# TensorE takes a step's logits ahead of its shared parts, and one part behind the ranks; four groups' statistics move behind group 1's routing

## The chip, the cores and the metric

One NeuronCore of a Trainium2 chip runs the whole program in one launch. The metric is the device time of an execution in microseconds (us); all times below are us unless marked otherwise. The engines are PE (TensorE, matmuls; PEld is its weight load), DVE (VectorE), ACT (ScalarE), POOL (GpSimd) and SP (SyncE, here a DMA queue). Each takes its own instructions in the order of the program and waits on semaphores for the others.

## The reference

x is 4096 tokens of 128 values (16 x 256 x 128). Three sublayers follow each other: a mixture of experts at half weight, a decaying scan between two circular convolutions, and the same mixture of experts again, with the same weights.

```python
def ffn(x_):                                   # x_ is 4096 x 128
    logits = x_ @ router.T                     # 8 experts
    onehot = one_hot(argmax(logits))           # one expert for each token
    y  = sum over e of onehot[:, e] * ((silu(x_ @ gate[e].T) * (x_ @ up[e].T)) @ down[e].T)
    ys = (silu(x_ @ w_gate_s.T) * (x_ @ w_up_s.T)) @ w_down_s.T      # shared expert, every token
    return y + ys
x = x + 0.5 * ffn(layernorm(x))
x = x + attn(layernorm(x))    # x + gate * circ_corr(scan(circ_conv(x, bind)), unbind)
x = x + 0.5 * ffn(layernorm(x))
```

All data are float32. A hidden width is 256, so the gate and up projections of one expert are two halves of 128 each.

## The kernel before

The 4096 tokens are 32 tiles of 128, held as 8 groups of 4 tiles (512 tokens); a group g has its columns in every buffer. Each of the two mixtures (f = 0 and f = 1) has a routing stage, which walks over the groups in steps k = 0 to 7, and an expert stage over blocks of 128 tokens sorted by expert.

A step k of the routing stage does the following for group k. PE multiplies the turned rows by the router (`logits`, L899). DVE finds the best expert (`choose`, L648 to L654; `chosen` is the one-hot choice). PE counts with small matmuls which place each token has among those of its expert (`ranks`, L918 to L926). DVE makes row numbers from them (`place_rows`, L663 and L667, tile `slot`). POOL then sends the four tiles with four indirect DMAs, the scatters (L349), to the buffer `dispatched`. In the same step ACT normalizes the next group (`norm`, L430), PE turns it (`turn`, L860, into one PSUM bank), and ACT copies the turned bank out (`evac_rows`, L445, tile `xnT`), which the next step's logits read.

The shared expert fills the gaps. For each group it has three parts: (g, 0) and (g, 1) are the two halves of gate and up (PE L874, then `silu` on ACT L454, then a product on DVE L623), and (g, DOWN) is the down projection (PE L882, then an addition on DVE L591). The list SHARED_PARTS sets their order, two to a step. I call the first part of a step A and the second B:

| step k | 1 | 2 | 3 | 4 | 5 | 6 | 7 |
|---|---|---|---|---|---|---|---|
| A | (0,0) | (1,0) | (1,1) | (1,DOWN) | (3,0) | (3,1) | (3,DOWN) |
| B | (0,1) | (0,DOWN) | (2,0) | (2,1) | (2,DOWN) | (4,0) | (4,1) |

The order within a step is written out by hand for each engine, in a function `front(f, k)` of its own. On PE it was: A, logits, B, turn of group k+1, ranks. On ACT, which the change leaves alone, it is: `evac_rows` of group k, `norm` of group k+1, silu of A, silu of B. The silu of a step's B is thus ahead of the copy that the next step's logits wait for.

In the second mixture (f = 1) the step also carries the scan. On PE, behind the logits, stands the product of the scanned rows with `mix` (L905, waits for DVE's scan L603), and at the end of the step the turn of group k+3 for the scan. On DVE the step is: scan of group k+2, the addition of returned expert rows (L591), `choose`, A's product, the addition of the retrieved rows (`add_retrieved`, L610), the statistics of that group (L550 to L561), `place_rows`, B's product. POOL has two reciprocal square roots (L338) ahead of a step's four scatters.

Behind step 7 DVE makes the tables of the expert blocks (`pads_behind` L736, then from `n_up` L749 to `tab_row` L777); five more shared parts stand ahead of the first expert matmul on PE (L951).

In the first mixture the mean and variance of groups 4 to 7 (`stats_of`) were taken on DVE in step 0 and step 1, because their load of x (`x_in[3]`) lands late. Newton steps in step 2 then make their reciprocal square roots.

Of the kernel before, what the change touches and what calls it, by code (L numbers as in the profile page):

```python
# [22 lines left out]
G = NT // TPG  # L23
# [29 lines left out]
LATE_ROWS = 4  # L53
# [7 lines left out]
def build(nc, x_in, gu_in, dn_in, router_in, bind_in, unbind_in, gate_in, decay_in, out):  # L61
# [6 lines left out]
    with ExitStack() as ctx:  # L68
# [152 lines left out]
        def valid(k):  # L221
            return 0 <= k < G
# [317 lines left out]
        def _(dve):  # L540
# [128 lines left out]
            def front(f, k):  # L669
                n, q = f * G + k, k % 2  # L670

                kind, later = ("f", G - 1 if k == 1 else G) if f == 0 else ("a", k + 4)
                if f == 0 and k == -AHEAD:
                    dve.wait_ge(x_in[0], 16)
                    stats_of("f", 0, 0)
                if f == 0 and k == 1 - AHEAD:
                    dve.wait_ge(x_in[1], 16)
                    stats_of("f", 1, 1)
                if f == 0 and k == 2 - AHEAD:
                    dve.wait_ge(x_in[2], 16)  # L680
                    stats_of("f", 2, 2)
                    stats_of("f", 3, 3)
                if valid(k):
                    root = f == 0 and k == 2
                    choose(n, q, kind, later, later, root)
                    if root:
                        for i in range(ROUTE_STEPS - 2, NEWTON_STEPS):
                            newton_step(i)
                for g, part in parts_at(k, 0):
                    shared(f, g, part)  # L690
                if f == 1 and valid(k + 2):
                    add_retrieved(k + 2)
                    stats_of("f", n + 2, k + 2)
                if valid(k):
                    place_rows(n, k, q)
                if f == 0 and k == 0:
                    dve.wait_ge(x_in[3], 16)
                    for late in range(G - LATE_ROWS, G - 1):
                        stats_of("f", late, late)
                if k == G - 1:  # L700
                    pads_behind(f)
                for g, part in parts_at(k, 1):
                    shared(f, g, part)
# [150 lines left out]
        def _(pe):  # L854
# [31 lines left out]
            def front(f, k):  # L886
                n, q = f * G + k, k % 2
                if n == 1:
                    pe.wait_ge(shared_in, 16 * 2)
                for g, part in parts_at(k, 0):  # L890
                    shared(f, g, part)
                if valid(k):
                    if n == 0:
                        pe.wait_ge(router_ready, 16)
                        pe.wait_ge(const_made, N_CONST)
                    pe.wait_ge(xnT_ready, n + 1)
                    wait_pos(pe, route, n * ROUTE_STEPS)
                    for t in range(TPG):
                        last = nc.tensor.matmul(rt[:, t * E:(t + 1) * E], xnT[:, k, t * P:(t + 1) * P], routerT[:],  # L899
                                                start=True, stop=True)  # L900
                    last.then_inc(logits, 1)
                if f == 1 and valid(k + 2):
                    pe.wait_ge(scan_done, k + 3)
                    for t in range(TPG):
                        last = nc.tensor.matmul(tp["a"][:, t * C:(t + 1) * C], scanned[:, q, t * P:(t + 1) * P],  # L905
                                                mix[:], start=True, stop=True)
                    last.then_inc(mixed, 1)
                for g, part in parts_at(k, 1):
                    shared(f, g, part)
                if valid(k + 1):  # L910
                    turn("f", n + 1, xn, k + 1, xnT_ready)
                if valid(k):

                    pe.wait_ge(route, n * ROUTE_STEPS + ROUTE_STEPS - 1)
                    if k == G - 1:
                        count_all()
                    ranks = by_tile(rt[:, RANK])
                    nc.tensor.matmul(ranks, before[:], chosen[:, q, 0:TPG, :], start=True, stop=False)  # L918
                    for t in range(TPG - 1):
                        nc.tensor.matmul(ranks[:, t + 1:TPG, :], ones[:],  # L920
                                         chosen[:, q, t:t + 1, :].to_broadcast([P, TPG - 1 - t, E]),
                                         start=False, stop=False)
                    nc.tensor.matmul(ranks, ones[:], chosen[:, q, TPG:TPG + 1, :].to_broadcast([P, TPG, E]),
                                     start=False, stop=False)

                    nc.tensor.matmul(ranks, ones[:], region[:].unsqueeze(1).to_broadcast([P, TPG, E]),  # L926
                                     start=False, stop=True).then_inc(ranked, 1)
                if f == 1 and valid(k + 3):
                    turn("a", k + 3, xa, 1 - q, x2_done)

# [110 lines left out]
```

## Time and profile before

| what | value |
|---|---|
| median of 3 runs | 297.3 (297.2 to 298.74) |
| the profiled execution | 297.33 |
| its span, first to last instruction | 295.6 |
| busy: PE, DVE, ACT, POOL | 254.9, 189.0, 160.5, 178.7 |
| mean granted clock of PE | 0.961 |

The profiled execution has 1.7 outside its span and stands at the median of the runs. The busy times are sums over stages with different limits; which engine ends last has to be read from each stage. The stages lie in the span about as follows: routing of the first mixture to 60, its experts from 66 to 127, the scan and the routing of the second mixture to 210, its experts from 216.

### The profile page before, as it was taken

Reading aid. Unit: us, or ns where it says so; the run is one execution under the profiler, and the core shown is the slowest. Engines: PE = TensorE matmul, PEld = TensorE weight load, DVE = VectorE, ACT = ScalarE, POOL = GpSimd, SP = SyncE. Lnnn points to the kernel's source line nnn. Section 1 sums busy time; section 2 is a strip of 40 time slices with the busy share of each in tenths; the row PEclk is TensorE's granted clock in tenths of the full one; section 3 lists DMA queues with packets and bytes.
Section 4 is the critical chain, followed back from the end, with each engine's and each line's share of the span. In section 5 each row is a group of like instructions: output and inputs, shape, how many; then the busy total and the mean of one; then the engine's idle time right before and its main releaser. Section 6 shows DMA issues by size and latency. Waiting matters only on the chain.

```text
span 295.6 us, 6436 instructions
## 1 busy us (share of the span) xinstructions
PE 254.9 (86%) x1788; PEld 211.0 (71%) x1788; DVE 189.0 (64%) x734; ACT 160.5 (54%) x374; POOL 178.7 (60%) x260
## 2 busy tenths in 40 slices
PE   0799999969999999985589988999779999999940
PEld 0557777648999999845466767766369999999520
DVE  4695665864555555448996999867625566565362
ACT  2705545145767767326497877750447767775100
POOL 6555677722777777723457788877307758887400
PEclk9999999999999999997676999999999999999995
DMA  6970111323344321147000001112323434311297
GB/s 187 332 300 27 48 55 59 95 79 74 102 111 107 105 81 47 45 130 185 0 1 27 29 28 38 49 45 83 96 64 104 107 94 111 90 54 48 65 303 237
DMA packets 34996, 28.42 MB, mean 96 GB/s; under 512 B 4784, under 2 KB 31792, under 8 KB 34704
## 3 DMA queue, kind: packets, MB, share of 16 engines
q1 hardware_dynamic: 25328, 16.06, 19.7%
q0 software_dynamic: 4544, 9.45, 9.7%
q10 hardware_dynamic: 5088, 2.50, 2.9%
q8 instruction: 14, 0.23, 0.4%
q14 instruction: 22, 0.18, 0.2%
HBM read 15.37 MB, written 12.62 MB: 95 GB/s over the span
## 4 chain that ended last, share of the span: by engine, by line
POOL 33%; PE 22%; issue 19%; DMA 10%; DVE 9%; ACT 2%; SPq 2%; POOLq 0%; DVEq 0%; ACTq 0%
POOL dispatched L349 15%; POOL returned L378 12%; PE bank L951 10%; PE bank L959 4%; PE bank L874 4%; DMA ey<-returned 4%; POOL scale_f L338 2%; DMA xres<-in_x 2%; POOL token L372 2%; DMA dispatched<-xn,slot 2%; DMA returned<-ey,token 2%; DVE st_f L550 1%; DMA xs<-dispatched 1%; SPq L308 1%; PE bank L899 1%
## 5 line engine op out<-in xcount | busy, mean ns | idle before, releaser
L378 POOL DMA_INDIRECT returned<-ey,token x78 | 76.8, 985 | 32.8 <-issue 17.8
L951 PE MATMUL bank<-xsT,wgu 128*128 128x128 f32 x624 | 83.0, 276 | 2.4 <-ACT xsT L497 2.4
L349 POOL DMA_INDIRECT dispatched<-xn,slot x64 | 63.5, 992 | 24.6 <-issue 17.7
L951 PEld LDWEIGHTS bank<-xsT,wgu 128*128 128x128 f32 x624 | 75.7, 192 | 3.4 <-ACT xsT L497 1.7
L874 PE MATMUL bank<-xnT,gu 128*128 128x512 f32 x128 | 66.7, 649 | 3.6 <-DVE hs L623 2.8
L805 DVE COPY ey<-bank 128x128 f32<-128x128 f32 x78 | 22.7, 292 | 45.6 <-PE bank L959 45.6
L481 ACT ACTIVATE wgu<-gu 128x512 f32 x78 | 48.3, 623 | 4.1 <-issue 3.9
L454 ACT ACTIVATE sg<-bank 128x512 f32<-128x512 f32 x32 | 18.9, 592 | 54.7 <-PE bank L874 47.3
L959 PE MATMUL bank<-wdn,eh 128*128 128x128 f32 x312 | 47.5, 276 | 0.5 <-DVE eh L800 0.5
L503 ACT ACTIVATE eg<-bank 128x256 f32<-128x256 f32 x78 | 29.8, 383 | 32.6 <-PE bank L951 32.4
L959 PEld LDWEIGHTS bank<-wdn,eh 128*128 128x128 f32 x312 | 40.9, 192 | 0.9 <-DVE eh L800 0.9
L874 PEld LDWEIGHTS bank<-xnT,gu 128*128 128x128 f32 x128 | 23.5, 203 | 23.5 <-issue 22.3
L882 PEld LDWEIGHTS bank<-dn,hs 128*128 128x128 f32 x256 | 31.0, 196 | 9.5 <-DVE hs L623 8.1
L882 PE MATMUL bank<-dn,hs 128*128 128x128 f32 x256 | 32.8, 282 | 4.7 <-DVE hs L623 4.7
L800 DVE TENSOR_TENSOR eh<-eg,bank 128x256 f32<-128x256 f32 x78 | 32.1, 411 | 5.9 <-ACT eg L503 5.9
L430 ACT ACTIVATE xn<-xres,shift_f,scale_f 128x128 f32<-128x128 f32 x64 | 26.3, 483 | 15.7 <-POOL shift_f L342 15.7
L623 DVE TENSOR_TENSOR hs<-sg,bank 128x512 f32<-128x512 f32 x32 | 21.8, 682 | 13.0 <-ACT sg L454 12.8
L786 DVE COPY wdn<-dn 128x256 f32 x78 | 23.6, 303 | 3.0 <-issue 3.0
L899 PEld LDWEIGHTS bank<-routerT,xnT 128*128 128x128 f32 x128 | 18.6, 215 | 7.3 <-issue 6.9
L860 PE MATMUL bank<-ident,xn 128*128 128x128 f32 x64 | 12.7, 319 | 7.7 <-POOL before L405 7.5
L860 PEld LDWEIGHTS bank<-ident,xn 128*128 128x128 f32 x64 | 9.4, 163 | 13.8 <-POOL before L405 7.5
L899 PE MATMUL bank<-routerT,xnT 128*128 128x8 f32 x128 | 17.5, 263 | 0.9 <-ACT xnT L445 0.8
(102 smaller groups left out, 282.7 us busy)
## 6 DMA issues: line engine op xcount, KB each, us to landing
xs<-dispatched SPq DMA_DIRECT2D x80, 66.0 KB, 1.9
ey<-returned SPq DMA_DIRECT2D x16, 256.0 KB, 5.7
gu<-in_gu SPq DMA_DIRECT2D x1, 2048.0 KB, 11.3
out<-xres ACTq DMA_DIRECT2D x8, 256.0 KB, 4.2
returned<-ey,token POOLq DMA_INDIRECT x78
dn<-in_dn SPq DMA_DIRECT2D x1, 1024.0 KB, 11.7
dispatched<-xn,slot POOLq DMA_INDIRECT x64, 2.3
dispatched<-pads SPq DMA_DIRECT2D x10, 66.0 KB
```

The lines of the kernel that those rows point to most:

```text
L349: nc.gpsimd.indirect_dma_start(dispatched[:, :], bass.IndirectOffsetOnAxis(slot[:, i:i + 1], 0), xn[:, i, :], None, bounds_check=last_row) ...
L378: nc.gpsimd.indirect_dma_start(returned[:, :], bass.IndirectOffsetOnAxis(token[:, b:b + 1], 0), ey[:, b, :], None, bounds_check=last_back) ...
L430: nc.scalar.activation(dst[:, at * TPG + t, 0:C], xres[:, i, :], ACT.Identity, bias=shift[kind][:, i:i + 1], scale=scale[kind][:, i:i + 1] ...
L481: nc.scalar.activation(wgu[:, b % WR, :], tile(gu, expert_of(digits[0], b)), ACT.Copy).then_inc(blk_wgu, 1)
L503: nc.scalar.activation(eg[:, b % WR, :], bank[4 + b % WR][:, 0:H], ACT.Silu).then_inc(blk_silu, 1)
L786: nc.vector.tensor_copy(wdn[:, b % WR, :], tile(dn[:].rearrange("p e h c -> p e (h c)"), expert_of(digits[0], b)))
L800: nc.vector.tensor_tensor(eh[:, b % WR, :], eg[:, b % WR, :], bank[4 + b % WR][:, H:2 * H], ALU.mult).then_inc(blk_mul, 1)
L874: last = nc.tensor.matmul(ps[:], gu[:, SHARED, at:at + P], xnT[:, g, :], start=True, stop=True)
L882: last = nc.tensor.matmul(o_ps[:, t * C:(t + 1) * C], hs[:, n % 2, h, t * P:(t + 1) * P], dn[:, SHARED, h, :], start=(h == 0), stop=(h == ...
L899: last = nc.tensor.matmul(rt[:, t * E:(t + 1) * E], xnT[:, k, t * P:(t + 1) * P], routerT[:], start=True, stop=True)
L951: last = nc.tensor.matmul(bank[4 + b % WR][:, i * P:(i + 1) * P], wgu[:, b % WR, i * P:(i + 1) * P], xsT[:, b // 2 % 2, b % 2, :], start=T ...
L959: last = nc.tensor.matmul(y_of(b), eh[:, b % WR, h * P:(h + 1) * P], wdn[:, b % WR, h * C:(h + 1) * C], start=(h == 0), stop=(h == HH - 1))
```

## The change

On PE, the logits of a step now come first (with the product by `mix`, where there is one); then A, then the turn and the ranks, and B behind the ranks. In step 1 of the first mixture both parts stand behind the ranks. On DVE, only step 1 of the first mixture changes, and step 0's three sets of statistics move: group 4's are taken between the instructions of step 1's `choose`, groups 5 and 6's behind its `place_rows`, then A's product, then group 7's. ACT, POOL and SP have the same instructions in the same order.

```diff
 # DVE
-                kind, later = ("f", G - 1 if k == 1 else G) if f == 0 else ("a", k + 4)
+                kind, later = ("f", G - LATE_ROWS if k == 1 else G) if f == 0 else ("a", k + 4)
...
                 if valid(k):
+                    if n == 1:
+                        dve.wait_ge(x_in[3], 16)
                     root = f == 0 and k == 2
                     choose(n, q, kind, later, later, root)
...
-                for g, part in parts_at(k, 0):
-                    shared(f, g, part)
+                if n != 1:
+                    for g, part in parts_at(k, 0):
+                        shared(f, g, part)
...
-                if f == 0 and k == 0:
-                    dve.wait_ge(x_in[3], 16)
-                    for late in range(G - LATE_ROWS, G - 1):
+                if n == 1:
+                    for late in range(G - LATE_ROWS + 1, G - 1):
                         stats_of("f", late, late)
+                    for g, part in parts_at(k, 0):
+                        shared(f, g, part)
+                    stats_of("f", G - 1, G - 1)
 # PE
-                for g, part in parts_at(k, 0):
-                    shared(f, g, part)
                 if valid(k):
...
-                for g, part in parts_at(k, 1):
-                    shared(f, g, part)
+                if n != 1:
+                    for g, part in parts_at(k, 0):
+                        shared(f, g, part)
                 if valid(k + 1):
                     turn("f", n + 1, xn, k + 1, xnT_ready)
...
+                if n == 1:
+                    for g, part in parts_at(k, 0):
+                        shared(f, g, part)
+                for g, part in parts_at(k, 1):
+                    shared(f, g, part)
                 if f == 1 and valid(k + 3):
                     turn("a", k + 3, xa, 1 - q, x2_done)
```

PE before, step 3 of the first mixture and the head of step 4 (`xnT,gu` is a gate part, `dn,hs` a DOWN part, `routerT,xnT` the logits, `ident,xn` the turn, `chosen,before` the first of the ranks):

```order
L874 MATMUL bank<-xnT,gu 128x512 x2
L899 MATMUL bank<-routerT,xnT 128x8 x4
L874 MATMUL bank<-xnT,gu 128x512 x2
L860 MATMUL bank<-ident,xn 128x128 x4
L918 MATMUL bank<-chosen,before 128x32
L920 MATMUL bank<-chosen,ones 128x24
L920 MATMUL bank<-chosen,ones 128x16
L920 MATMUL bank<-chosen,ones 128x8
L923 MATMUL bank<-chosen,ones 128x32
L926 MATMUL bank<-region,ones 128x32
L882 MATMUL bank<-dn,hs 128x128 x8
L899 MATMUL bank<-routerT,xnT 128x8 x4
```

The same stretch of PE now:

```order
L902 MATMUL bank<-routerT,xnT 128x8 x4
L879 MATMUL bank<-xnT,gu 128x512 x2
L865 MATMUL bank<-ident,xn 128x128 x4
L922 MATMUL bank<-chosen,before 128x32
L924 MATMUL bank<-chosen,ones 128x24
L924 MATMUL bank<-chosen,ones 128x16
L924 MATMUL bank<-chosen,ones 128x8
L927 MATMUL bank<-chosen,ones 128x32
L930 MATMUL bank<-region,ones 128x32
L879 MATMUL bank<-xnT,gu 128x512 x2
L902 MATMUL bank<-routerT,xnT 128x8 x4
L887 MATMUL bank<-dn,hs 128x128 x8
```

Between B's last matmul and the logits of step 4, where step 4's A stood, nothing stands any more.

ACT in the same stretch, the same before and now: the copy of group 3's turned rows (`xnT`), the norm of group 4, step 3's two silus (`sg`, the second is B's), the copy of group 4's turned rows:

```order
L445 ACTIVATE xnT<-bank 128x512 [waits turned_f]
L430 ACTIVATE xn<-xres,shift_f,scale_f 128x128 [waits late_rstd]
L430 ACTIVATE xn<-xres,shift_f,scale_f 128x128 x3
L454 ACTIVATE sg<-bank 128x512 [waits mult_done,gu_done] x2
L445 ACTIVATE xnT<-bank 128x512 [waits turned_f]
```

The copy that the logits wait for stood and stands behind B's silu; only what PE has to do meanwhile has moved.

PE in the second mixture, step 2 before (`mix,scanned` is the product that waits for the scan):

```order
L874 MATMUL bank<-xnT,gu 128x512 [waits mult_done,xnT_ready]
L874 MATMUL bank<-xnT,gu 128x512
L899 MATMUL bank<-routerT,xnT 128x8 [waits route,xnT_ready]
L899 MATMUL bank<-routerT,xnT 128x8 x3
L905 MATMUL bank<-mix,scanned 128x128 [waits scan_done]
```

and now:

```order
L902 MATMUL bank<-routerT,xnT 128x8 [waits route,xnT_ready]
L902 MATMUL bank<-routerT,xnT 128x8 x3
L908 MATMUL bank<-mix,scanned 128x128 [waits scan_done]
L908 MATMUL bank<-mix,scanned 128x128 x3
L879 MATMUL bank<-xnT,gu 128x512 [waits mult_done,xnT_ready]
```

A gate part that stood ahead of the wait for the scan stands behind it.

## Rows read from the trace of the kernel before

**Rows 1.** The page, chain of work that ended last, shares of the span by line.
```profile
POOL dispatched L349 15%; POOL returned L378 12%; PE bank L951 10%; PE bank L959 4%; PE bank L874 4%; DMA ey<-returned 4%; POOL scale_f L338 2%; DMA xres<-in_x 2%; POOL token L372 2%; DMA dispatched<-xn,slot 2%; DMA returned<-ey,token 2%; DVE st_f L550 1%; DMA xs<-dispatched 1%; SPq L308 1%; PE bank L899 1%
```

**Rows 2.** Timeline, POOL's scatters: start, duration, engine, line; idle before, and its releaser.
```profile
24.27 0.97 POOL L349 DMA_INDIRECT dispatched<-xn,slot  x1 [4.54 <-DVE slot L667]
...
30.32 0.97 POOL L349 DMA_INDIRECT dispatched<-xn,slot  x1 [1.27 <-DVE slot L667]
...
59.88 0.97 POOL L349 DMA_INDIRECT dispatched<-xn,slot  x1 [0.30 <-issue]
```

**Rows 3.** Timeline, PE and DVE in steps 0 to 2 of the first mixture.
```profile
13.78 3.76 PE L874 MATMUL bank<-xnT,gu 128*128 128x512 f32 x4
13.97 0.19 DVE L663 TENSOR_TENSOR place<-bank,chosen 128x32 f32<-128x32 f32 x1 [0.44 <-PE bank L926]
...
15.91 0.87 DVE L550 BATCH_NORM_STATS2 st_f<-xres 128x6 f32<-128x128 f32 x4
...
17.33 1.72 PE L899 MATMUL bank<-routerT,xnT 128*128 128x8 f32 x8
...
20.58 0.22 DVE L654 TENSOR_REDUCE chosen<-chosen 128x8 bf16<-128x40 bf16 x1
...
23.69 1.88 PE L874 MATMUL bank<-xnT,gu 128*128 128x512 f32 x4
...
25.41 0.95 PE L899 MATMUL bank<-routerT,xnT 128*128 128x8 f32 x8
```

**Rows 4.** Timeline, PE and ACT in step 6 of the first mixture.
```profile
46.17 0.95 PE L899 MATMUL bank<-routerT,xnT 128*128 128x8 f32 x8
...
46.98 1.96 PE L874 MATMUL bank<-xnT,gu 128*128 128x512 f32 x4
...
48.78 0.60 PE L860 MATMUL bank<-ident,xn 128*128 128x128 f32 x4
...
48.98 0.60 ACT L454 ACTIVATE sg<-bank 128x512 f32<-128x512 f32 x1 [1.96 <-PE bank L874]
...
49.37 2.03 PE L882 MATMUL bank<-dn,hs 128*128 128x128 f32 x16
...
49.47 0.59 ACT L445 ACTIVATE xnT<-bank 128x512 f32<-128x512 f32 x1
...
51.24 0.96 PE L899 MATMUL bank<-routerT,xnT 128*128 128x8 f32 x8
```

**Rows 5.** The page, costliest groups: DVE's product of a gate part (busy, mean ns).
```profile
L623 DVE TENSOR_TENSOR hs<-sg,bank 128x512 f32<-128x512 f32 x32 | 21.8, 682 | 13.0 <-ACT sg L454 12.8
```

**Rows 6.** Timeline, first mixture's tables and the shared part behind them.
```profile
55.28 0.16 DVE L749 TENSOR_SCALAR n_up<-bank 128x8 int32<-128x8 f32 x1
...
60.92 1.95 PE L874 MATMUL bank<-xnT,gu 128*128 128x512 f32 x4 [1.43 <-DVE hs L623]
```

**Rows 7.** Timeline, DVE and PE in steps 1, 2 and 5 of the second mixture.
```profile
160.26 0.19 DVE L648 TENSOR_REDUCE top<-bank 128x4 f32<-128x32 f32 x1 [2.24 <-issue]
...
162.95 0.68 DVE L610 TENSOR_TENSOR xres<-bank,xres 128x512 f32<-128x512 f32 x1
...
167.32 1.16 PE L905 MATMUL bank<-mix,scanned 128*128 128x128 f32 x8 [0.47 <-DVE scanned L603]
...
168.31 1.95 PE L882 MATMUL bank<-dn,hs 128*128 128x128 f32 x16
...
170.56 0.68 DVE L610 TENSOR_TENSOR xres<-bank,xres 128x512 f32<-128x512 f32 x1
...
191.34 0.68 DVE L610 TENSOR_TENSOR xres<-bank,xres 128x512 f32<-128x512 f32 x1
```

**Rows 8.** Timeline, second mixture, PE: turn of the second tile for the experts.
```profile
214.96 0.33 PE L940 MATMUL bank<-ident,xs 128*128 128x128 f32 x1 [0.92 <-DMA xs<-dispatched]
```

**Rows 9.** Windows: length; busy PE, PEld, DVE, ACT, POOL; PEclk (granted clock), DMA, GB/s.
```profile
151.00:152.00 1.00, 0.93 (x8) 0.93 (x8) 0.97 (x5) 0.64 (x2) 0.60 (x1) 1.00 0.00 0
...
153.00:154.00 1.00, 0.99 (x8) 0.65 (x8) 0.94 (x8) 1.00 (x3) 0.11 (x1) 0.50 0.00 0
```

## The prediction

> **What bounds the kernel now.** I read the chain of work that ended last first: POOL's scatters hold 15% of the span [rows 1], and all of them lie in the two routing stages, so these stages are where the change has to be weighed. Next I read POOL in the timeline [rows 2]. In the first mixture it stands idle twice, 4.54 us before group 1's first scatter and 1.27 before group 2's, each time for DVE's row numbers. From 30.32 on it never waits: the 24 scatters of groups 2 to 7 start at 30.32 to 59.88, 29.56 / 23 = 1.285 each, or 5.14 for a group. So the most that can be won there is the two waits less the 0.30 that POOL needs between scatters anyway: 4.24 + 0.97 = 5.2.
>
> Then I read the timeline of PE over one step [rows 4]. From the logits of step 6 to those of step 7 it is 51.24 - 46.17 = 5.07: logits 0.81, A (a gate part) 1.80, turn and ranks 0.59, B (a DOWN part) 1.87. PE has no gap in it. The reader should see that PE's 5.07 is nearly POOL's 5.14. A step that grows by more than a few tenths makes POOL wait again, and what is lost in several steps adds up.
>
> **First mixture, the gain at the start.** Before, group 1's logits stood behind (0, 0), a part of 17.33 - 13.78 = 3.55 us [rows 3]. That part took twice what a gate part takes later (1.80), so PE ran there at the lower of its two clock levels. Now the logits follow group 0's ranks. They must wait until DVE has read these (13.97 + 0.19), so they start at about 14.3. From logits to the end of `choose` took 20.80 - 17.33 = 3.47, with the same interleaved statistics and the same clock, so group 1's choice is there at 17.8 and its row numbers about 1 us later, before POOL is through with group 0's scatters at 24.27 - 4.54 = 19.73. The 4.54 wait goes.
>
> **First mixture, group 2.** Behind the ranks, from about 18.0, PE does (0, 0) and (0, 1). At the lower clock both end at 18.0 + 7.1 = 25.1. Before, PE was slow in (0, 1) and fast in the part at 23.69; if the clock returns at the same time, near 23.2, they end at about 24.1; if it returns as early as the start of (0, 1), at 23.35. Now the new wait comes in. Group 2's logits read the copy that ACT makes of the turned rows, and on ACT that copy stands behind the silu of (0, 1). From the rows of step 6 [rows 4]: the silu starts 2.00 after a gate part's start (48.98 - 46.98), the copy 0.49 after the silu (49.47), and it ends 0.59 later, 3.08 after the part's start. PE is through with the part after 1.80. So whenever B is a gate part, PE stands idle for 3.08 - 1.80 = 1.3 us. Before, A of the next step filled this time. Group 2's logits then come at 24.1 + 1.3 = 25.4, against 25.41 [rows 3]: no change, bounds 24.65 and 26.4 from the two ends above. What is behind the logits (choice, Newton steps, row numbers) is as before, so POOL's second wait remains, and the time won on group 1 is waited away there: gain 0, bounds -0.8 and +1.0.
>
> The moved statistics I cost at nothing. Groups 5 and 6 run on DVE while PE does (0, 0), group 7 while it does (0, 1); DVE then waits for group 2's logits in any case. The wait for the late load of x stands later than before, where the late groups' statistics ran at 15.91 already. If that cover went, group 2 would be late by what is left of one set, whose four statistics take 0.87 and their aggregation about as much.
>
> **First mixture, steps 3 to 7.** B is a gate part in steps 3, 4 and 6, so the logits of steps 4, 5 and 7 each come 1.3 later: 3.9 by step 7. PE's other work per step is the same. POOL, with its 5.14 against PE's 5.07, can't make it up. DVE is not late on its own: it gets the choice done under A.
>
> **First mixture, the end.** Before, step 7's B, (4, 1), ran between its logits and its ranks; now it runs behind the last ranks, and DVE still makes its product ahead of the tables. Before, tables came 55.28 - 51.24 = 4.04 after the logits of step 7 [rows 6, 4]. Now it is logits 0.81, (3, DOWN) 1.87, ranks 0.15, then 2.00 to the silu, 0.60 for it, 0.68 for the product [rows 5]: 6.1. That adds 2.1. Behind the tables PE waits for DVE (1.43 at 60.92), so the shared parts there and the first expert matmul behind them move along [rows 6]. Sum of the first mixture: 0 + 3.9 + 2.1 = +6.0.
>
> **Second mixture.** DVE's step goes by `add_retrieved`: 162.95, 170.56, ..., 191.34 for steps 1 to 5, 28.4 for four steps [rows 7]. Now A stands on PE behind the product with `mix`, which waits for DVE's scan, and DVE needs A's result ahead of `add_retrieved`. The loop closes: from `add_retrieved` over the scan to the `mix` product 167.32 - 162.95 = 4.37, product 168.31 - 167.32 = 0.99, gate part to silu 2.00, silu 0.60, product 0.68 [rows 4, 5]: 8.6 for steps 2, 3 and 5. Step 4 has a DOWN part, 1.87 and 0.2 to its end in place of part and silu: 8.1. Four steps are 33.9, 5.5 more than before. Step 1 starts it: DVE can take its choice up to 2.24 earlier (its wait before 160.26), but its next product now needs (0, 0), which PE does last instead of first. I take 0, bounds -2.2 and +1.75 (a gate part at the lower clock less one at the higher). The end costs 2.1 as above, less the 0.92 for which PE waited there for data anyway [rows 8]: +1.2. Sum of the second mixture: +6.7.
>
> **The clock.** At 151 to 152 PE did only logits and `mix` products, 0.93 busy, at full granted clock; at 153 to 154 the granted clock was 0.50 [rows 9]. Now every step from 2 to 5 has such a stretch of some 4 us between B and A: turn, copy, logits, the wait for the scan, product. I take one of the five A parts of steps 1 to 5 at half clock: +1.75; none is the lower bound, all five the upper. The page "TensorE: Matmul & The Clock Gate" of the Trainium skill, section "Why this matters for your kernels", says that gaps between bursts of matmuls in mid-kernel throw PE back to its slow clock, which speaks against this change; by it all five parts would be slow, and that is the second rival below. These rows show one such fall; none shows it for gaps of this very mix.
>
> **The sum**, against the profiled execution's 297.33, which is the median: 297.33 + 6.0 + 6.7 + 1.75 = 311.8. Expert stages and the final stores have the same instructions and no new wait: 0.
>
> **Rivals.**
> 1. Only the first mixture loses. In the second, POOL has a step of its own (four scatters and two square roots); if DVE's product comes before it needs it, because the choice runs 2 us earlier, the loop doesn't close. 297.33 + 6.0 = 303.3. Against it: 8.6 is made of durations that follow each other on different engines, and the step of before, 7.6, had PE and DVE nearly full.
> 2. PE's clock falls in every step. All five A parts at 1.75 more: 297.33 + 6.0 + 6.7 + 8.75 = 318.8. For it, rows 9; against it, PE still has two heavy parts in each step.
> 3. The change gains: the copy comes in time, and PE's step stays within POOL's 5.14, so that POOL's two waits are won for good: 297.33 - 5.2 = 292.1. It decides where the copy ends before PE has finished B. That needs it ahead of B's silu on ACT, and the program has it behind.
> 4. The gain at the start and the new waits cancel in the first mixture, and the second is bound by POOL as before: 297.
>
> **How the numbers follow.** Forecast 311.8, chance 0.56, its own range 307 to 316 (step 1's and group 2's bounds). Rival 1: 0.14. Rival 2: 0.20. Rival 3: 0.06. Rival 4: 0.04. The range 303 to 319 leaves out rivals 3 and 4 and the far side of rival 2, about 2 in 10. About 0.5%, 1.5 us, is what a measurement of this kernel can tell from no change. Faster 0.06, same 0.04, slower 0.90.
>
> **What would show it.** In the trace of after: group 1's scatters directly behind group 0's, and a wait of some 5 us ahead of group 2's; PE waiting about 1.3 for ACT's copy ahead of the logits of groups 2, 4, 5 and 7 in the first mixture and POOL waiting in steps 4 to 7; the tables' first instruction near 61; in the second mixture `add_retrieved` every 8.6 with DVE waiting for ACT's silu ahead of A's product. The prediction is wrong if PE's logits don't wait for the copy, or if DVE's wait for A's product is absent, or if PE's granted clock falls much oftener than once.

## The result, and the profile after

| | before | after |
|---|---|---|
| median of the runs made side by side | 297.41 | 319.31 |
| ratio, 95% interval | | 1.0763 [1.0701, 1.0825] |
| the profiled execution, its span | 297.33, 295.6 | 319.95, 318.2 |
| mean granted clock of PE | 0.961 | 0.924 |
| first expert matmul of the first and of the second mixture | 66.27, 215.96 | 74.59, 238.48 |

One execution of the changed kernel took 660.69, twice the others (318.48 to 319.95); the median of 319.31 counts it, the ratio does not. The change made the kernel 7.6% slower by the ratio. The median is 7.5 above the forecast of 311.8 and 0.3 above the upper end of the range; the three others lie on both sides of that end.

The first expert matmuls, two of the kernel before and two of the changed one, in the timeline of PE:

```profile
66.27 2.02 PE L951 MATMUL bank<-xsT,wgu 128*128 128x128 f32 x16 [0.68 <-ACT xsT L497]
215.96 2.02 PE L951 MATMUL bank<-xsT,wgu 128*128 128x128 f32 x16 [0.68 <-ACT xsT L497]
...
74.59 2.05 PE L960 MATMUL bank<-xsT,wgu 128*128 128x128 f32 x16 [1.09 <-DVE xres L591]
238.48 1.72 PE L960 MATMUL bank<-xsT,wgu 128*128 128x128 f32 x13 [1.14 <-DVE xres L591]
```

By these, the first mixture lost 74.59 - 66.27 = 8.3, and from there to the same point in the second it took 163.9 where it took 149.7, so 14.2 were lost there. What follows costs 0.1 more. The first expert stage is as long as before (58.2 against 58.3). Thus the two routing stages hold the whole loss.

The page of the changed kernel, the chain that ended last by engine and by line, against [rows 1]:

```profile
PE 40%; DVE 16%; issue 15%; POOL 14%; DMA 6%; ACT 4%; SPq 2%; DVEq 1%; POOLq 0%; ACTq 0%
PE bank L879 13%; POOL returned L378 11%; PE bank L960 9%; PE bank L887 6%; PE bank L902 4%; PE bank L968 4%; DMA ey<-returned 3%; DVE st_f L550 3%; PE bank L908 2%; POOL token L372 2%; DMA xres<-in_x 2%; ACT sg L454 2%; DVE xres L610 2%; D
```

The scatters (L349), 15% of the chain before, have no entry in the line; in their place stand PE's gate and DOWN parts (L879, L887) and the engines that hand results to each other. So POOL no longer sets the end of the routing stages. POOL's timeline in the first mixture, the scatters that waited for DVE's row numbers, against [rows 2]:

```profile
28.93 0.97 POOL L349 DMA_INDIRECT dispatched<-xn,slot  x1 [4.67 <-DVE slot L667]
...
42.19 0.97 POOL L349 DMA_INDIRECT dispatched<-xn,slot  x1 [3.26 <-DVE slot L667]
49.28 0.97 POOL L349 DMA_INDIRECT dispatched<-xn,slot  x1 [2.29 <-DVE slot L667]
...
60.73 0.97 POOL L349 DMA_INDIRECT dispatched<-xn,slot  x1 [1.56 <-DVE slot L667]
```

Group 1's wait of 4.54 is gone. A wait of 4.67 stands ahead of group 2, and POOL then waits 3.26, 2.29 and 1.56 ahead of groups 4, 5 and 7, where before it never did; groups 3 and 6, with 0.39 and 0.31, are hardly over the 0.30 that lies between scatters anyway. The reason is in the timeline of PE and ACT at the end of step 3 and in step 4, against [rows 4]:

```profile
33.16 1.96 PE L879 MATMUL bank<-xnT,gu 128*128 128x512 f32 x4
35.16 0.60 ACT L454 ACTIVATE sg<-bank 128x512 f32<-128x512 f32 x1 [2.62 <-PE bank L879]
35.65 0.59 ACT L445 ACTIVATE xnT<-bank 128x512 f32<-128x512 f32 x1
...
36.30 1.06 PE L902 MATMUL bank<-routerT,xnT 128*128 128x8 f32 x8 [1.18 <-ACT xnT L445]
37.21 3.27 PE L887 MATMUL bank<-dn,hs 128*128 128x128 f32 x16
40.27 1.05 PE L865 MATMUL bank<-ident,xn 128*128 128x128 f32 x4
```

Read it downwards: B ends, ACT takes its silu, only then the copy, and PE stands still for 1.18 until the copy is there. The same 1.18 stands ahead of the logits at 44.45 and 55.96, and 0.96 ahead of those at 23.95. What the prediction did not have is the next row: the DOWN part behind the wait took 3.27, where one takes 1.95 to 2.03. The windows of these microseconds (columns as in [rows 9]) show the granted clock:

```profile
32.00:33.00 1.00, 0.34 (x5) 0.11 (x2) 0.86 (x6) 0.54 (x1) 0.69 (x2) 1.00 0.00 0
...
35.00:36.00 1.00, 0.12 (x1) 0.00 (x0) 0.21 (x1) 0.84 (x2) 0.69 (x2) 1.00 0.23 72
36.00:37.00 1.00, 0.70 (x7) 0.70 (x7) 0.47 (x1) 1.00 (x4) 0.69 (x2) 1.00 0.08 30
37.00:38.00 1.00, 1.00 (x10) 1.00 (x10) 0.54 (x3) 0.77 (x3) 0.69 (x2) 0.88 0.12 38
38.00:39.00 1.00, 1.00 (x7) 1.00 (x7) 0.64 (x4) 0.00 (x0) 0.93 (x1) 0.50 0.20 68
...
40.00:41.00 1.00, 1.00 (x7) 1.00 (x6) 0.48 (x1) 0.00 (x0) 0.00 (x0) 0.50 0.00 0
```

PE was busy for 0.34 of the microsecond from 32 (its ranks waited 0.66 for DVE's choice), fully from 33 to 35, for 0.12 and 0.70 of the next two, and then its granted clock fell from 1.00 to 0.50, its lower level of 1.2 GHz, and stayed there through the DOWN part.

In the second mixture the timeline shows one whole turn of the loop that the prediction describes, against [rows 7]:

```profile
172.75 0.68 DVE L610 TENSOR_TENSOR xres<-bank,xres 128x512 f32<-128x512 f32 x1
...
175.27 1.03 PE L902 MATMUL bank<-routerT,xnT 128*128 128x8 f32 x8 [0.96 <-DVE place L663]
175.86 1.21 DVE L603 TENSOR_TENSOR_SCAN scanned<-keep,bank 128x512 f32<-128x512 f32 x1
...
177.13 1.57 PE L908 MATMUL bank<-mix,scanned 128*128 128x128 f32 x8 [0.82 <-DVE scanned L603]
...
178.49 3.20 PE L879 MATMUL bank<-xnT,gu 128*128 128x512 f32 x4
...
181.72 0.60 ACT L454 ACTIVATE sg<-bank 128x512 f32<-128x512 f32 x1 [3.64 <-PE bank L879]
...
182.35 0.69 DVE L623 TENSOR_TENSOR hs<-sg,bank 128x512 f32<-128x512 f32 x1 [2.49 <-ACT sg L454]
...
182.95 0.68 DVE L610 TENSOR_TENSOR xres<-bank,xres 128x512 f32<-128x512 f32 x1
```

From `add_retrieved` to the next is 10.20: 4.38 to the product with `mix`, 1.36 to A, 3.23 to its silu, 0.63 to DVE's product, 0.60 to `add_retrieved`. DVE waits 2.49 for the silu. The forecast for the same links was 4.37, 0.99, 2.00, 0.60 and 0.68, in all 8.64. So the loop is the one described, and what is too long in it is what PE does. Windows:

```profile
174.00:175.00 1.00, 0.31 (x3) 0.07 (x1) 0.93 (x9) 1.00 (x3) 0.00 (x0) 1.00 0.00 0
...
176.00:177.00 1.00, 0.30 (x3) 0.21 (x2) 1.00 (x2) 1.00 (x4) 0.76 (x3) 1.00 0.00 0
177.00:178.00 1.00, 0.87 (x6) 0.88 (x7) 0.97 (x5) 1.00 (x3) 0.70 (x2) 0.85 0.00 0
178.00:179.00 1.00, 1.00 (x5) 0.82 (x4) 1.00 (x8) 0.08 (x1) 0.89 (x1) 0.50 0.21 68
```

The granted clock falls at the product with `mix`, reads 0.50 in the microsecond in which A begins, and is back at 1.00 when B runs. A is slow in all of steps 1 to 5: the gate parts at 168.33, 178.49, 188.66 and 208.11 took 3.16 to 3.30, and the DOWN part at 198.83 took 3.28. But step 1's A was slow in the kernel before, too:

```profile
155.37 3.62 PE L874 MATMUL bank<-xnT,gu 128*128 128x512 f32 x4
```

There the granted clock was 0.50 from 153 to 159. So four slow parts are new, those of steps 2 to 5.

### The profile page after: what moved, and what is told of

Same layout as the page of the kernel before. It is cut to its first block, busy times and chain, and to the rows that moved or that the text cites. A ratio compares the mean times of both kernels' runs of the same rounds, so it can differ in the third digit from the quotient of the medians.

```text
span 318.2 us, 6435 instructions
## 1 busy us (share of the span) xinstructions
PE 266.0 (84%) x1788; PEld 217.9 (68%) x1788; DVE 189.8 (60%) x734; ACT 160.5 (50%) x374; POOL 178.8 (56%) x260
## 4 chain that ended last, share of the span: by engine, by line
PE 40%; DVE 16%; issue 15%; POOL 14%; DMA 6%; ACT 4%; SPq 2%; DVEq 1%; POOLq 0%; ACTq 0%
PE bank L879 13%; POOL returned L378 11%; PE bank L960 9%; PE bank L887 6%; PE bank L902 4%; PE bank L968 4%; DMA ey<-returned 3%; DVE st_f L550 3%; PE bank L908 2%; POOL token L372 2%; DMA xres<-in_x 2%; ACT sg L454 2%; DVE xres L610 2%; DVE xres L591 1%; DMA returned<-ey,token 1%
## 5 line engine op out<-in xcount | busy, mean ns | idle before, releaser
L349 POOL DMA_INDIRECT dispatched<-xn,slot x64 | 63.3, 989 | 30.1 <-issue 16.5
L879 PE MATMUL bank<-xnT,gu 128*128 128x512 f32 x128 | 69.0, 673 | 4.2 <-DVE hs L623 3.4
L623 DVE TENSOR_TENSOR hs<-sg,bank 128x512 f32<-128x512 f32 x32 | 21.9, 684 | 38.9 <-ACT sg L454 38.9
L879 PEld LDWEIGHTS bank<-xnT,gu 128*128 128x128 f32 x128 | 25.2, 215 | 27.4 <-issue 26.3
L887 PEld LDWEIGHTS bank<-dn,hs 128*128 128x128 f32 x256 | 34.3, 214 | 8.8 <-DVE hs L623 7.9
L887 PE MATMUL bank<-dn,hs 128*128 128x128 f32 x256 | 36.4, 302 | 4.1 <-DVE hs L623 4.1
L902 PEld LDWEIGHTS bank<-routerT,xnT 128*128 128x128 f32 x128 | 17.9, 217 | 17.7 <-ACT xnT L445 13.9
L902 PE MATMUL bank<-routerT,xnT 128*128 128x8 f32 x128 | 19.0, 275 | 12.2 <-ACT xnT L445 7.3
L338 POOL TENSOR_TENSOR scale_f<-var_f,minus_half 128x4 f32<-128x4 f32 x12 | 12.2, 1015 | 19.2 <-DVE minus_mean_f L561 19.2
L865 PEld LDWEIGHTS bank<-ident,xn 128*128 128x128 f32 x64 | 10.5, 180 | 15.0 <-POOL before L405 7.4
```

The lines of the kernel that those rows point to most:

```text
L349: nc.gpsimd.indirect_dma_start(dispatched[:, :], bass.IndirectOffsetOnAxis(slot[:, i:i + 1], 0), xn[:, i, :], None, bounds_check=last_row) ...
L879: last = nc.tensor.matmul(ps[:], gu[:, SHARED, at:at + P], xnT[:, g, :], start=True, stop=True)
L887: last = nc.tensor.matmul(o_ps[:, t * C:(t + 1) * C], hs[:, n % 2, h, t * P:(t + 1) * P], dn[:, SHARED, h, :], start=(h == 0), stop=(h == ...
```

## The experiments

Each kernel is compared with the kernel before on the same chip (medians 296.55 to 296.77 there). A profile shows a single execution; where that one is far from its kernel's median, the text says so.

**1. The copy taken earlier.** ACT copies the next group's turned rows ahead of B's silu, in both mixtures; everything else as in the changed kernel.

```diff
 # ACT, front(f, k)
-                if valid(k):
+                if valid(k) and k < 2:
                     evac_rows(n)
...
+                if 1 <= k < G - 1:
+                    evac_rows(n + 1)
                 for g, part in parts_at(k, 1):
                     shared(f, g, part)
```

> ACT copies the next group's turned rows ahead of the silu of the step's B, in both mixtures; nothing else differs from the changed kernel. Theory (in the first mixture PE waits for that copy, 1.2 us at each of groups 4, 5 and 7, and the lower clock in two DOWN parts follows from these waits): the first mixture's steps go back to 5.07, its first expert matmul from 74.6 to about 68.5, the second mixture stays within 1 us, whole time about 313. Rival A (the logits are late for something else, such as DVE's row numbers): no change, 319. Rival B (the copy also sets the second mixture's loop): about 306.

Measured: 309.18 (308.65 to 310.4), ratio 1.0415 [1.0348, 1.0483]. The first expert matmul came at 66.07, so all of the first mixture's 8.3 was back, more than the 6 expected. The timeline of PE and ACT in steps 3 and 4:

```profile
31.30 0.59 ACT L445 ACTIVATE xnT<-bank 128x512 f32<-128x512 f32 x1
...
31.98 1.96 PE L881 MATMUL bank<-xnT,gu 128*128 128x512 f32 x4
33.78 0.95 PE L904 MATMUL bank<-routerT,xnT 128*128 128x8 f32 x8
33.98 0.60 ACT L454 ACTIVATE sg<-bank 128x512 f32<-128x512 f32 x1 [2.09 <-PE bank L881]
34.59 2.03 PE L889 MATMUL bank<-dn,hs 128*128 128x128 f32 x16
```

The copy (31.30) is done before B starts, the logits have no wait, and the DOWN part takes 2.03. One edit that touches only the wait took the wait and the fall of the clock away together. The fall in step 4 needed the wait for the copy: PE's wait for DVE's choice ahead of the ranks was still there (0.61 at 31.82), and the clock stayed up. The second mixture took 161.3 from first expert to first expert, 2.6 less than in the changed kernel, where a change within 1 was expected: 1.7 of it up to step 1 and 1.0 behind step 5. Its loop did not move, with `add_retrieved` 10.0 on average over four steps, as in the changed kernel.

**2. The second mixture in PE's order of before.** The changed kernel, with A ahead of the logits and B ahead of the turn for f = 1.

```diff
 # PE, front(f, k)
+                if f == 1:
+                    for g, part in parts_at(k, 0):
+                        shared(f, g, part)
...
                 if n != 1:
-                    for g, part in parts_at(k, 0):
+                    for g, part in parts_at(k, f):
                         shared(f, g, part)
...
-                for g, part in parts_at(k, 1):
-                    shared(f, g, part)
+                if f == 0:
+                    for g, part in parts_at(k, 1):
+                        shared(f, g, part)
```

> In the second mixture PE has its order of before (A, logits, product by mix, B, turn, ranks, turn for the scan); the first mixture is that of the changed kernel. Theory (each mixture loses on its own, the first 8.3, the second about 14): 297.4 + 8.3 = 305.7. Rival (the second mixture's loss is handed on by the first, or by the statistics): above 310.

Measured: 306.95 (306.56 to 308.07), ratio 1.0322 [1.0258, 1.0386]; first expert matmuls at 74.65 and 225.92. The profiled execution took 308.07; in it the first mixture keeps its loss of 8.4, and the second takes 151.3 against 149.7 before. So the two mixtures' losses are in the main separate; 1.6 in that one execution is not accounted for.

**3. A ahead of the wait for the scan.** In the second mixture PE does logits, A, the product with `mix`, turn, ranks, B.

```diff
 # PE, front(f, k), behind the logits
+                if f == 1:
+                    for g, part in parts_at(k, 0):
+                        shared(f, g, part)
                 if f == 1 and valid(k + 2):
                     pe.wait_ge(scan_done, k + 3)
...
-                if n != 1:
+                if f == 0 and n != 1:
```

> In the second mixture PE does logits, A, product by mix, turn, ranks, B: A only steps out from behind the wait for the scan. Theory (the second mixture's loop runs over scan, product by mix, A, silu, DVE's product): the loop opens, add_retrieved comes every 7.7 to 8 instead of 10.2, whole time 306 to 309. Rival (the lower clock of A alone makes the loss, wherever A stands): 316 or more.

Measured: 308.49 (304.34 to 308.95), ratio 1.0382 [1.0317, 1.0447]. The profiled execution is the fastest, 304.34. In it the second mixture took 149.5 and every part ran at full clock; the timeline of PE and DVE:

```profile
170.69 1.96 PE L879 MATMUL bank<-xnT,gu 128*128 128x512 f32 x4
172.49 1.05 PE L911 MATMUL bank<-mix,scanned 128*128 128x128 f32 x8
...
174.12 0.69 DVE L623 TENSOR_TENSOR hs<-sg,bank 128x512 f32<-128x512 f32 x1
174.72 0.68 DVE L610 TENSOR_TENSOR xres<-bank,xres 128x512 f32<-128x512 f32 x1
```

A lies under DVE's scan again, and DVE's product has no wait. In this execution A's place behind the scan is thus the cause of the second mixture's loss, its clock included. The median lies 308.5 - 304.3 = 4.2 above it; where the other executions lose these 4.2, this one profile can't show.

**4. Spare matmuls in the gaps.** A matmul of 128x512 (two in the trace's counting), whose result the next part overwrites, ahead of the logits and another ahead of the product with `mix`, in steps 1 to 5 of the second mixture. The order of the work stays.

```diff
 # PE
+            def fill(f, k):
+                for g, part in parts_at(k, 0) if f == 1 and k <= 5 else []:
...
+                    nc.tensor.matmul(ps[:], ident[:], gu[:, SHARED, :], start=True, stop=True)
...
+                    fill(f, k)
                     pe.wait_ge(xnT_ready, n + 1)
...
+                fill(f, k)
                 if f == 1 and valid(k + 2):
                     pe.wait_ge(scan_done, k + 3)
```

> Two spare 128x512 matmuls of some 0.9 us each in every step 1 to 5 of the second mixture, one ahead of the wait for DVE's row numbers and one ahead of the wait for the scan, into the bank that A overwrites later: they add work that no result needs. Theory (A runs at half clock because PE has a light stretch ahead of it): the granted clock stays up, a gate part's four matmuls take 1.96 instead of 3.2, add_retrieved comes every 8.7, whole time about 313. Rival (the loop is set by waits, not by the clock, and PE has no room): no change or up to 2 us slower, 319 to 321.

Measured: 313.16 (311.3 to 314.13), ratio 1.0518 [1.0441, 1.0596]: more work, and some 6 less than the changed kernel (313.16 against 319.31, and 16.4 above the kernel before against 21.9). The timeline of PE and DVE in one step:

```profile
174.97 1.10 PE L898 MATMUL bank<-gu,ident 128*128 128x512 f32 x2
175.94 1.16 PE L919 MATMUL bank<-mix,scanned 128*128 128x128 f32 x8
176.93 1.88 PE L879 MATMUL bank<-xnT,gu 128*128 128x512 f32 x4
...
179.48 0.69 DVE L623 TENSOR_TENSOR hs<-sg,bank 128x512 f32<-128x512 f32 x1 [0.81 <-ACT sg L454]
180.09 0.68 DVE L610 TENSOR_TENSOR xres<-bank,xres 128x512 f32<-128x512 f32 x1
```

A takes 1.88 again, and `add_retrieved` comes at 171.57, 180.09 and 188.61, every 8.52. That is the loop forecast without a slow A (8.64). The clock's share of a step is 10.20 - 8.52 = 1.7, measured apart from the order and with the spare matmuls paid. Step 1 gained nothing: its A took 1.91, and still the stretch up to its `add_retrieved` was as long as in the changed kernel (98.2 from the first expert matmul).

**5. Three mends together.** Edits 1 and 3, and DVE makes the product of step 7's B between `block_experts` and `tables`, so that the tables' first part doesn't wait for it.

```diff
 # DVE (with the edits of 1 and 3)
-                for g, part in parts_at(k, 1):
+                for g, part in parts_at(k, 1) if k < G - 1 else []:
                     shared(f, g, part)
...
                 block_experts()
+                for g, part in parts_at(G - 1, 1):
+                    shared(f, g, part)
                 tables()
```

> The changed kernel with three mends: ACT copies the next group's rows ahead of B's silu; in the second mixture A stands ahead of the product by mix; DVE makes the product of step 7's B between the two halves of the tables' instructions instead of ahead of them. Theory (these three waits are the whole loss, and what was won at group 1 then reaches the end in part): the first mixture's first expert matmul at about 64.3 against 66.27 before, the second mixture as before or 1 to 2 us less, whole time about 293. Rival A (PE's own work sets the routing stage, so nothing is won): 297, within 1. Rival B (there are further waits of the same size): 300 or more.

Measured: 302.18 (298.13 to 303.0), ratio 1.0100 [1.0041, 1.0160]; not the gain that was expected. Both losses' places are mended, and the kernel is still not faster. In the profiled execution (302.21) the first mixture gained 0.7 (first expert matmul 65.53) and the second took 153.8. Two parts there ran at a granted clock of 0.50: step 1's A at 157.43 with 3.76, which was slow in the kernel before, too, and, newly, the DOWN part of step 4. The timeline of PE:

```profile
180.93 1.03 PE L906 MATMUL bank<-routerT,xnT 128*128 128x8 f32 x8 [1.14 <-DVE place L665]
181.81 3.56 PE L891 MATMUL bank<-dn,hs 128*128 128x128 f32 x16
```

The wait ahead of it is one for DVE's row numbers, which A covered as long as it stood ahead of the logits. The tables' stretch, from `n_up` to the first expert matmul, was 2.2 longer.

**6 and 7. One half of the change at a time**, on the kernel before: only B behind the ranks (6), only the logits ahead of A (7).

```diff
 # 6: PE of before
-                for g, part in parts_at(k, 1):
-                    shared(f, g, part)
                 if valid(k + 1):
...
+                for g, part in parts_at(k, 1):
+                    shared(f, g, part)
                 if f == 1 and valid(k + 3):
 # 7: PE of before
-                for g, part in parts_at(k, 0):
-                    shared(f, g, part)
                 if valid(k):
...
-                for g, part in parts_at(k, 1):
+                for g, part in parts_at(k, 0) + parts_at(k, 1):
                     shared(f, g, part)
```

> The kernel before with one part of the change alone: B stands behind the ranks, in both mixtures; logits stay behind A, the statistics stay. Theory (the copy hides under the next A, but the ranks now wait for DVE's choice, some 1.2 us a step, with only the turn between; the second mixture's loop stays open): first mixture about 7 late, whole time 303 to 306. Rival (B's place alone makes the whole loss): 314 or more.

> The kernel before with the other part alone: logits, and the product by mix, ahead of A; B ahead of the turn and the ranks as before; the statistics stay. Theory (the copy now follows the turn with only the ranks to hide it, some 0.75 a step in the first mixture; in the second A stands behind the wait for the scan, 10 or more in all): 308 to 314. Rival (the logits' place is harmless, only B's makes the loss): 296 to 299.

Measured: 306.31 (304.45 to 311.31, profiled 304.45), ratio 1.0329 [1.0271, 1.0386] for 6, and 312.91 (310.54 to 313.84), ratio 1.0533 [1.0481, 1.0584] for 7. Neither half is harmless, and each has a wait of its own. In 6 nothing is left on PE between the turn and the ranks, so PE waits for DVE's choice in each step:

```profile
34.23 0.19 PE L916 MATMUL bank<-chosen,before 128*128 128x32 bf16 x1 [1.00 <-DVE chosen L654]
...
40.41 0.19 PE L916 MATMUL bank<-chosen,before 128*128 128x32 bf16 x1 [0.98 <-DVE chosen L654]
```

The first mixture's steps are 6.1 long, and its first expert matmul comes at 72.77 (+6.5). In 7 the turn stands behind both parts, so that the copy and with it the next logits come late (0.60 on PE at 40.29, after a copy at 39.64). The first mixture loses 2.6, and the second, where A again stands behind the scan, 13.4.

**8. Step 1 alone.** The changed kernel's step 1 and DVE order, PE's order of before in all other steps.

> The changed kernel's DVE order and its step 1 of the first mixture on PE, all other steps on PE as before. Theory (POOL's early start is waited away, since PE's parts set the steps; at most the 1 us by which group 2's logits come earlier is left): group 1's scatters at 20, whole time 295.5 to 297 beside 296.8 before. Rival (POOL's two waits are worth what they measure): 5 us less than before, 291.6.

Measured: 297.73 (296.06 to 301.0), ratio 1.0043 [1.0018, 1.0068]: no gain, but 0.4% more; the first expert matmul of the profiled execution (296.29) came at 66.16, 0.1 earlier than before. POOL's timeline:

```profile
30.50 0.97 POOL L349 DMA_INDIRECT dispatched<-xn,slot  x1 [5.95 <-DVE slot L667]
```

Group 1's wait of 4.54 and group 2's of 1.27 have become one of 5.95 ahead of group 2. Taking group 1 earlier only moves the wait by one group.

**9 to 11. Can a mended form win?** Kernel 9 has the changed first mixture with edit 1 (first mixture alone) and the DVE edit of 5 (first mixture alone), and the second mixture of before. Kernel 10 has edit 1 (first mixture alone) and edit 3. Kernel 11 is the kernel before with edit 1 (first mixture alone) and nothing else.

> First mixture with the copy ahead of B's silu and step 7's product between the expert blocks and the tables, second mixture with PE's order of before. If the loss sits in the two places found (the copy, the second mixture's loop) and nowhere else, the first expert matmul comes near 65.5 (the three-mend kernel's), the second mixture takes 149.7 from there as before, and the time is 0.7 below before: 296 to 297.5. If the early copy also costs the later stages something: 300 or more.

> Copy early in the first mixture alone, A ahead of the product with mix in the second; DVE as in the changed kernel, so step 7's product stays ahead of the tables in both mixtures. If the second mixture's 4 us in the three-mend kernel came from the copy being early there or from the moved product of step 7: first expert 66.1, second mixture 149.5, 296.5 to 298. If they come from A standing behind the logits there: 300 to 302, as the three mends.

> The kernel before with one edit: ACT copies the turned rows of the next group ahead of B's silu in the first mixture. My theory: PE has A to do between B and the logits, so the copy is not waited for and being early brings nothing; the turn stands behind B on PE there, so B's silu now waits for the turn and the copy, some 1.2 later, which DVE's product follows: 296.5 to 299. If the copy was on before's path all the same: up to 5 less, 292.

| kernel | median | ratio, 95% interval |
|---|---|---|
| 9 | 296.86 (295.46 to 299.34) | 1.0019 [0.9982, 1.0056] |
| 10 | 300.73 (298.06 to 303.94) | 1.0140 [1.0071, 1.0209] |
| 11 | 296.66 (294.98 to 299.47) | 1.0019 [0.9978, 1.0060] |

Kernel 9 closes the account: with the first mixture mended and the second in its order of before, the kernel is back at the time of before. Its first expert matmul comes 1.07 earlier than before (65.20), which is too little to measure. POOL's timeline says why it is not the 5.2 of the third rival:

```profile
28.39 0.97 POOL L349 DMA_INDIRECT dispatched<-xn,slot  x1 [4.07 <-DVE slot L669]
```

Of the two waits of before (5.81 together) 4.07 are still there, one group later. Kernel 11 shows that taking the copy earlier brings nothing as long as PE has a part to do meanwhile; its place became a cost only with the change. Kernel 10 leaves something open: in its profiled execution, the fastest (298.06), the first expert matmul of the second mixture comes at 216.35, 0.4 later than before, but the kernel's median is 2.7 above that execution, and lies where it was expected if A's place behind the logits costs the rest (300 to 302). The kernel before, too, ranged from 294.77 to 299.75 on that chip, so a single profile settles little here. With A behind the logits, PE waits 0.4 to 1.0 for DVE's `place_rows` ahead of the logits in four of the steps (0.99 at 155.93), a wait that A covered before, and 0.7 to 1.2 for the copy in three others. In the profile of experiment 5 such a wait was followed by a slow part (181.81); the one profile of kernel 10 has no slow part in the second mixture. That these waits make the slower executions, by the clock or otherwise, is an argument and not shown.

## Why the prediction missed: the direction and the waits were right, the clock was mis-sized

The terms against what the two profiled executions show (the first expert matmuls and the named rows, after less before):

| term | forecast | measured | from |
|---|---|---|---|
| group 2's logits | 0 (-0.8 to +1.0) | -1.46 | 23.95 against 25.41 |
| first mixture, logits of group 2 to group 7 | +3.9 | +6.18 | 55.96 - 23.95 against 51.24 - 25.41 |
| from there to the tables | +2.1 | +3.76 | 63.76 - 55.96 against 4.04 |
| tables to first expert matmul | 0 | -0.16 | 10.83 against 10.99 |
| second mixture, up to step 1 | 0 (-2.2 to +1.75) | +1.48 | 172.75 - 74.59 against 162.95 - 66.27 |
| second mixture, four steps | +5.5 | +11.54 | 212.68 - 172.75 against 28.39 |
| second mixture, end | +1.2 | +1.18 | 238.48 - 212.68 against 215.96 - 191.34 |
| second expert stage and stores | 0 | +0.10 | what is left of 22.62 |
| clock, not placed | +1.75 | in the rows above | |
| sum | +14.45 | +22.62 | |

**The step that failed** is the clock's term, "I take one of the five A parts of steps 1 to 5 at half clock: +1.75". All five were slow, four of them newly: the prediction had read the fall at 153 [rows 9], but not that the clock stayed down to 159, so that step 1's A was slow before as well. The second rival had all five slow, and it got 0.20 because "PE still has two heavy parts in each step"; that reason was wrong, since the clock fell between B of one step and A of the next. In the loop it cost 39.93 - 33.9 = 6.0 over four steps (1.6 a step, and experiment 4 measures 1.7). That the clock "falls much oftener than once" was one of the prediction's own signs of being wrong.

**The row up to step 1** (+1.48) stays open. The slow A doesn't explain it: A took less there than before (3.16 against 3.62). In experiment 4 A ran at 1.91, and the stretch was the same 98.2 (171.57 - 73.38); in experiment 1 A took 3.06, and the stretch was 96.5 (162.54 - 66.07), against 96.7 before.

**The clock in the first mixture** had no term at all. There it fell in step 4 (37.21: the turn came 3.06 after the DOWN part's start instead of 1.8, and took 0.45 more itself: 1.7 in all) and behind the logits of step 7 (DOWN 0.5 and gate part 1.1 longer: 1.6). Together the clock holds about 6.0 + 1.7 + 1.6 = 9.3 of the 22.6 where 1.75 was forecast, so the rest is 13.3, against 12.7 forecast for the waits alone. The second rival's 318.8 came close by luck: it placed all 8.75 in the second mixture, where 6.0 fell, and had nothing for the first, whose 3.3 were in part made up by group 2's earlier logits.

**Two readings that were wrong besides.** "DVE is not late on its own" fails in step 3, where PE waited 0.66 for its choice (32.99), most of what the first mixture's row has beyond the copies and the clock. And the first part of 3.55 was put down to the lower clock level, which the granted clock doesn't bear out (last section).

**What was right.** The wait for the copy, about 1.3 ahead of the logits of groups 4, 5 and 7: measured 1.18 each, and experiment 1 shows it by taking it away. For group 2 it was 0.96, but PE got through the two parts earlier than assumed. The time won on group 1 waited away at group 2: 4.67, and 5.95 in experiment 8. The loop of the second mixture, link by link but for PE's. The tables' 2.1 at the end of the second mixture: 6.20 from the logits of step 7, forecast 6.1. That the end's sum fits (+1.18) is in part luck: the logits of step 7 came 0.4 late, and behind the tables 1.4 was gained instead of 0.92. In the first mixture the tables came at 63.76 instead of near 61, in the main by the clock.

**What was not foreseen and cost nothing in the loop**: PE's logits wait for `place_rows` (0.96 at 175.27), since A no longer covers DVE's work. The product with `mix` behind them waits 0.82 for the scan anyway, so the path runs through the scan. In the forms with A between the logits and the product with `mix` it may be the wait that is left.

The page "TensorE: Matmul & The Clock Gate" of the Trainium skill, section "Why this matters for your kernels", warns of gaps between bursts of matmuls in mid-kernel. The trace agrees with that direction at both places: 0.12 and 0.31 busy shortly ahead of the falls to 0.50. It doesn't agree everywhere: 0.27 and 0.55 busy from 43 to 45 brought no fall. The rule was cited in the prediction and then weighed too lightly.

## What to carry to other kernels

When an edit moves work away from ahead of a wait, list every wait which that work covered, on its own engine and on those that feed it; here A covered the copy on ACT, the scan on DVE and DVE's row numbers all at once, and each came out as soon as A had moved. Price the new idle time twice on TensorE: the wait itself, and, as a risk, the next heavy part at the lower clock, because here the second held 9.3 of 22.6. And before shifting one group earlier in a pipeline, ask what its successor waits for: POOL's 4.54 only moved to the next group.

## What the runs showed of the hardware

- A short pause could bring the clock down, and the same pause elsewhere did not. In step 3 of the first mixture PE was fully busy from 33 to 35, had 0.12 and 0.70 in the next two microseconds, and ran at a granted clock of 0.50 from 38 on; with the wait for the copy removed (experiment 1) the DOWN part in its place took 2.03 again instead of 3.27. The same wait of 1.18 ahead of the logits at 44.45 was followed by no fall, and the gate part behind it took 1.96. Which pauses bring a fall, these runs don't settle.

```profile
43.00:44.00 1.00, 0.27 (x1) 0.00 (x0) 0.06 (x1) 0.69 (x2) 0.69 (x2) 1.00 0.20 68
44.00:45.00 1.00, 0.55 (x5) 0.55 (x5) 0.63 (x1) 1.00 (x3) 0.70 (x2) 1.00 0.00 0
```

- Work whose result is thrown away can pay for itself: experiment 4 issues two more matmuls of 128x512 in each of five steps and is some 6 faster than the changed kernel.
- The prediction put the slow first part (3.55) down to the lower clock level. The windows don't bear that out: in the changed kernel's first gate parts two matmuls start in a microsecond (18 to 19) and later four (22 to 23), and the granted clock reads 1.00 in both. Two in a microsecond is also the rate at 179 to 181, where it reads 0.50. So either the level was low and the granted clock doesn't show it, or something else held these matmuls; which, stays open.

```profile
18.00:19.00 1.00, 1.00 (x2) 0.35 (x2) 0.96 (x6) 0.00 (x0) 0.81 (x1) 1.00 0.99 411
...
22.00:23.00 1.00, 1.00 (x4) 0.38 (x2) 1.00 (x5) 0.19 (x1) 0.97 (x1) 1.00 0.20 68
```
